# First attention of a four-block kernel: head outputs sent through DRAM to the output projection, full-array products moved to steps 5, 13, 21 and 29

## The reference

```python
x = x + attn(layernorm(x), qkv_w, qkv_b, proj_w, proj_b)   # 16 batches of 512 tokens, C = 128

H, D = 16, 8
qkv = (x @ qkv_w + qkv_b).reshape(b, n, 3, H, D)
attn = softmax(einsum('bnhd,bmhd->bhnm', q, k) * D ** -0.5, axis=-1)
out = einsum('bhnm,bmhd->bnhd', attn, v).reshape(b, n, 128)
out = out @ proj_w + proj_b
```

## Time and profile before

| | us |
|---|---|
| median of 3 runs | 3264.02 (3258.78 to 3268.07) |
| the profiled execution's own time | 3287.01 |
| its span, first to last instruction | 3285.2 |
| mean granted clock of PE | 0.905 of 2.4 GHz |
| PE busy in the span | 2902.0 |
| DVE busy in the span | 2549.6 |
| ACT busy in the span | 1791.8 |
| POOL busy in the span | 919.2 |

### The profile page before, as it was taken

One profiled execution on the slowest core, in us unless ns is written; L12 is line 12 of the kernel. 1 busy time (PEld: TensorE's weight loads), 2 busy tenths in 40 slices (PEclk: granted clock), 3 DMA queues, 4 the chain that ended last, 5 costly groups with the idle time before them and its releaser, 6 DMA issues. The chain is left out here.

```text
span 3285.2 us, 47363 instructions
## 1 busy us (share of the span) xinstructions
PE 2902.0 (88%) x15778; PEld 1773.0 (54%) x15778; DVE 2549.6 (78%) x6662; ACT 1791.8 (55%) x3223; POOL 919.2 (28%) x885
## 2 busy tenths in 40 slices
PE   6999879999999998999976698899899999989753
PEld 4666534444444443666644565566566656556432
DVE  7998768989989871899967898776476687697765
ACT  3544307778877774445445455464345555655444
POOL 2212121211211101122101555565233323434233
PEclk9999958999999996999985789899899999999965
DMA  4434322222212201344420000000000000000000
GB/s 130 101 83 104 81 98 95 76 77 95 86 67 95 83 25 52 79 104 94 89 52 1 1 14 20 13 26 20 33 10 11 14 14 7 14 7 26 7 7 26
DMA packets 71611, 167.26 MB, mean 51 GB/s; under 512 B 8792, under 2 KB 9416, under 8 KB 67144
## 3 DMA queue, kind: packets, MB, share of 16 engines
q1 hardware_dynamic: 69192, 160.04, 17.0%
q10 hardware_dynamic: 2176, 4.19, 0.3%
HBM read 120.68 MB, written 43.52 MB: 50 GB/s over the span
## 5 line engine op out<-in xcount | busy, mean ns | idle before, releaser
L697 DVE TENSOR_REDUCE att_mx<-att_s 128x1 f32<-128x512 f32 x1024 | 636.9, 683 | 92.6 <-PE att_s L949 91.7
L874 ACT ACTIVATE att_pt<-att_t 128x512 f32<-128x512 f32 x1024 | 548.5, 603 | 183.7 <-PE att_t L959 181.4
L949 PE MATMUL att_s<-att_k,att_q 32*128 32x512 f32 x1024 | 333.1, 532 | 31.2 <-DVE att_mx L697 16.0
L970 PE MATMUL att_o<-att_pt,att_vx 128*32 128x256 f32 x4096 | 335.8, 414 | 10.5 <-ACT att_oT L880 9.6
L959 PE MATMUL att_t<-att_q,att_k 32*128 32x512 f32 x1024 | 321.1, 521 | 2.9 <-ACT att_pt L874 2.6
L959 PEld LDWEIGHTS att_t<-att_q,att_k 32*128 32x128 f32 x1024 | 135.2, 190 | 217.5 <-ACT att_pt L874 106.5
L949 PEld LDWEIGHTS att_s<-att_k,att_q 32*128 32x128 f32 x1024 | 143.6, 194 | 69.8 <-DVE att_mx L697 51.3
L460 ACT ACTIVATE ffnA_h<-ffnA_up,b 128x512 f32<-128x512 f32 x144 | 98.6, 686 | 131.5 <-PE ffnA_up L105 131.0
L460 ACT ACTIVATE ffnB_h<-ffnB_up,b 128x512 f32<-128x512 f32 x144 | 98.6, 686 | 130.5 <-PE ffnB_up L105 130.0
L970 PEld LDWEIGHTS att_o<-att_pt,att_vx 128*32 128x32 f32 x4096 | 92.1, 112 | 143.4 <-ACT att_pt L874 70.3
L1896 ACT ACTIVATE att1k_sq<-att1k_k 128x512 f32<-128x512 f32 x128 | 76.1, 595 | 167.1 <-PE att1k_k L105 167.0
(11 more groups left out here) (535 smaller groups left out, 7710.7 us busy)
## 6 DMA issues: line engine op xcount, KB each, us to landing
ffnA_weights<-ffnA_weights SPq DMA_DIRECT2D x128, 256.0 KB, 5.3
att_q<-att_spread_q SPq DMA_DIRECT2D x16, 1024.0 KB, 5.0
att_k<-att_spread_k SPq DMA_DIRECT2D x16, 1024.0 KB, 4.8
att_spread_q<-att_qhi SPq DMA_DIRECT2D x32, 256.0 KB, 2.5
att_spread_k<-att_khi SPq DMA_DIRECT2D x32, 256.0 KB, 4.0
twk_hi<-ffnB_weights SPq DMA_DIRECT2D x32, 256.0 KB, 4.0
twk_lo<-ffnB_weights SPq DMA_DIRECT2D x32, 256.0 KB, 5.2
tgk_hi<-ffnB_weights SPq DMA_DIRECT2D x32, 256.0 KB, 6.1
```

Source lines behind the costliest of these rows:

```text
L697: v.tensor_reduce(top[b % 2][:, t, h + n % 2:h + n % 2 + 1], sbanks[n % 3][:, :], AX, ALU.max, negate=True).then_inc(mx, 1)
L874: a.activation(pt[k % 8][:, n % 2, :], tbanks[n % 3][:, :], ACT.Exp, scale=scale).then_inc(p_, 1)
L949: pe.matmul(sbanks[n % 3][:, :], qb[b % 3][r, u, t * P:(t + 1) * P], kb[b % 3][r, u, :], start=True, stop=True).then_inc(s_, 1)
L970: last = pe.matmul(obank[j * BLOCK:(j + 1) * BLOCK, cols], vxb[b % 3][:, t, 4 * u + j, :], pt[(2 * g + j // 2) % 8][:, j % 2, cols], start ...
```

## The change

The outputs of a unit no longer go back to tokens through PE. SP writes ACT's copy (values and sums of four heads, 256 KB) to a DRAM tensor `kept_o`, four times for a batch. When all four are there, SP loads the sums of the 16 heads as 128x64 (`rec`) and the values as channels by tokens (`ocol`). DVE inverts the sums in step 23. SP writes the inverses to DRAM and loads them again, each row repeated for the 8 channels of its head (`spread_rec`). POOL multiplies `ocol` by it, and PE projects at step 29, `ended` following at step 30. Values are computed at step 21 in place of 17, ACT's copy of them at 22 in place of 18. In stretches that have no next batch, PE gets two 128x512 products of constants into `misc` at steps 5, 13 and 21, which nothing reads.

```diff
+INVERTED = 23
-        def divided(w):
-            ...
-            m = st.at(v.reciprocal(rc[:, :, :], ov[:, :, :, HDIM]))
-            v.tensor_tensor(o[:, :, 4 * u:4 * u + 4, :], ov[:, :, :, 0:HDIM], ..., ALU.mult).then_inc(on, 1)
+        def inverted_sums(b):
+            v.wait_ge(sums, 16 * (b + 1))
+            if b:
+                v.wait_ge(inverted, 16 * b)
+            v.reciprocal(rec[:, :], rec[:, :]).then_inc(inverse, 1)
 # vector: loop over n
-                if n == 8 and old: divided(UNITS * (m - 2) + 2)
-                if n == 16 and old: divided(UNITS * (m - 2) + 3)
+                if n == INVERTED and old: inverted_sums(m - 2)
-                if n == 24 and old: ended(m - 2)
-                if n == 26 and now: divided(UNITS * (m - 1))
-                if n == 31 and now: divided(UNITS * (m - 1) + 1)
+                if n == 30 and old: ended(m - 2)
 # pool
-        for b in range(groups):
-            normal(b)
-            spread(b)
+        def divided(b):
+            p.wait_ge(came, 16 * (b + 1))
+            p.wait_ge(divisor, 16 * (b + 1))
+            p.tensor_tensor(ocol[:, :], ocol[:, :], spread_rec[:, :], ALU.mult).then_inc(on, 1)
+        for m in range(-1, groups + 2):
+            if m + 1 < groups:
+                normal(m + 1)
+                spread(m + 1)
+            if m >= 2:
+                divided(m - 2)
 # sync
+        def outputs(w):
+            b, u = divmod(w, UNITS)
+            sp.wait_ge(oT, w + 1)
+            if u == 0 and b:
+                sp.wait_ge(came, 16 * b)
+                sp.wait_ge(sums, 16 * b)
+            sp.dma_start(kept_o[4 * u:4 * u + 4, :, :]..., oTb[w % 2][:, :]).then_inc(kept[w % 2], 16)
+        def gather(b):
+            for written in kept:
+                sp.wait_ge(written, 16 * UNITS // 2 * (b + 1))
+            sp.dma_start(rec[:, :], kept_o[:, HDIM, :]...).then_inc(sums, 16)
+            if b:
+                sp.wait_ge(fp, b)
+            sp.dma_start(ocol[:, :], kept_o[:, 0:HDIM, :]).then_inc(came, 16)
+        def invert(b):
+            sp.wait_ge(inverse, b + 1)
+            if b:
+                sp.wait_ge(divisor, 16 * b)
+            sp.dma_start(kept_rec..., rec[:, :]).then_inc(inverted, 16)
+            sp.wait_ge(inverted, 16 * (b + 1))
+            sp.dma_start(spread_rec[:, :], kept_rec.unsqueeze(1).to_broadcast([HEADS, HDIM, GROUP])).then_inc(divisor, 16)
+        for m in range(groups + 2):
+            new, old, now = m + 1 < groups, m >= 2, 1 <= m <= groups
+            if now: maxima(m - 1)
+            if old: outputs(UNITS * (m - 2) + 2)
+            if new: operand_q(m + 1)
+            if old: outputs(UNITS * (m - 2) + 3)
+            if new: operand_k(m + 1)
+            if old:
+                gather(m - 2)
+                invert(m - 2)
+            if now:
+                outputs(UNITS * (m - 1))
+                outputs(UNITS * (m - 1) + 1)
 # scalar
-                a.wait_ge(oTT, w - 1)
+                a.wait_ge(kept[w % 2], 16 * (w // 2))
-                if n == 18 and new: values(m + 1)
+                if n == 22 and new: values(m + 1)
-                if n == 22 and old: final(m - 2)
 # tensor
+    def kept_busy(m, n):
+        return m + 1 >= groups and n in (5, 13, 21) and STEPS * m + n - LAG < total
+        def constant(k):
+            misc_free(pe, "constant", k)
+            for _ in range(2):
+                pe.matmul(misc[:, :], K["spread"][:, 0, :], K["spread"][:, 0:4, :]..., start=True, stop=True)
-                if n == 7 and old: out(UNITS * (m - 2) + 2)
-                if n == 15 and old: out(UNITS * (m - 2) + 3)
-                if n == 17 and new: project_v(m + 1)
-                if n == 21 and old: final(m - 2)
-                if n == 23 and old: projected(m - 2)
-                if n == 25 and now: out(UNITS * (m - 1))
-                if n == 30 and now: out(UNITS * (m - 1) + 1)
+                if n == 21 and new: project_v(m + 1)
+                if kept_busy(m, n): constant(STEPS * m + n)
+                if n == 29 and old: projected(m - 2)
```

More of the change, by code:

```diff
@@ L599, in attn0 @@
     total = STEPS * groups
-    (var, root, normed, biased, xT, xc, qp, kp, qr, kr, ql, kl, vp, vx, s_, mx, mt, mT, mr, t_, p_, w_, oT, oTT, on,
-     fT, fc, fp, done) = signals(nc, ctx, name, "var root normed biased xT xc qp kp qr kr ql kl vp vx s mx mt mT mr t p w oT oTT"
-                                 " on fT fc fp done")
+    (var, root, normed, biased, xT, xc, qp, kp, qr, kr, ql, kl, vp, vx, s_, mx, mt, mT, mr, t_, p_, w_, oT, on,
+     fp, done) = signals(nc, ctx, name, "var root normed biased xT xc qp kp qr kr ql kl vp vx s mx mt mT mr t p w oT on fp done")
+    kept = signals(nc, ctx, name, "kept0 kept1")
+    came, sums, inverse, inverted, divisor = signals(nc, ctx, name, "came sums inverse inverted divisor")
     dq, dk, dm = [signals(nc, ctx, name, f"{n}0 {n}1 {n}2") for n in ("dq", "dk", "dm")]
@@ L624, in attn0 @@
     spread_m = nc.dram_tensor(name + "_spread_m", [4, BLOCK, GROUP], F32, kind="Internal").ap()
+    kept_o = nc.dram_tensor(name + "_kept_o", [HEADS, BLOCK, GROUP], F32, kind="Internal").ap()
+    kept_rec = nc.dram_tensor(name + "_kept_rec", [HEADS, GROUP], F32, kind="Internal").ap()
     xg = lambda b: X[:, b, :, :]
@@ L639, in uses_of_misc @@
                 yield "x", m + 1
-            if old:
-                yield "out", UNITS * (m - 2) + 2
-            if new:
                 yield "q", m + 1
                 yield "k", m + 1
+                yield "v", m + 1
+            for n in (5, 13, 21):
+                if kept_busy(m, n):
+                    yield "constant", STEPS * m + n
             if old:
[L646 to L650, removed]
                 yield "proj", m - 2
-            if now:
-                yield "out", UNITS * (m - 1)
-                yield "out", UNITS * (m - 1) + 1
     misc_uses = list(uses_of_misc())
@@ L672, in misc_free @@
                 pe.wait_ge(mr, k + 1)
[L673 to L676, removed]
             if kind == "proj":
@@ L747, in vector @@
                     maxima(m - 1)
[L748 to L751, removed]
+                if n == INVERTED and old:
+                    inverted_sums(m - 2)
                 if n == 20 and m + 2 < groups:
@@ L755, in vector @@
                     stats(m + 2, 2, TILES)
[L756 to L759, removed]
                 if n == 29 and m + 2 < groups:
                     moments(m + 2)
-                if n == 31 and now:
-                    divided(UNITS * (m - 1) + 1)
+                if n == 30 and old:
+                    ended(m - 2)
     def pool(p):
@@ L909, in scalar @@
                     raw_k(m + 1)
-                if n == 18 and new:
+                if n == 22 and new:
                     values(m + 1)
@@ L913, in scalar @@
                     out(UNITS * (m - 1))
-                if n == 22 and old:
-                    final(m - 2)
                 if n == 29 and now:
@@ L978, in maxima @@
             last.then_inc(mT, 1)
[L980 to L988, removed]
+        def constant(k):
+            misc_free(pe, "constant", k)
+            for _ in range(2):
+                pe.matmul(misc[:, :], K["spread"][:, 0, :], K["spread"][:, 0:4, :].rearrange("p c n -> p (c n)"), start=True, stop=True)
         def projected(b):
-            pe.wait_ge(fc, b + 1)
+            pe.wait_ge(on, b + 1)
             misc_free(pe, "proj", b)
@@ L1017, in tensor @@
                     turned(m + 1)
-                if n == 7 and old:
-                    out(UNITS * (m - 2) + 2)
                 if n == 9 and new:
@@ L1023, in tensor @@
                     project_k(m + 1)
-                if n == 15 and old:
-                    out(UNITS * (m - 2) + 3)
-                if n == 17 and new:
+                if n == 21 and new:
                     project_v(m + 1)
-                if n == 21 and old:
-                    final(m - 2)
-                if n == 23 and old:
+                if kept_busy(m, n):
+                    constant(STEPS * m + n)
+                if n == 29 and old:
                     projected(m - 2)
[L1032 to L1035, removed]
     with nc.Block() as block:
```

45 lines of the change are left out of this document (20 added, 25 removed).

## The result

| | before | after |
|---|---|---|
| median of the runs, us | 3262.47 (3258.78 to 3268.07, 4 runs) | 3314.99 (3314.22 to 3318.98, 4 runs) |
| profiled execution, us | 3287.01 | 3315.72 |
| span, us | 3285.2 | 3313.8 |

The ratio of the runs is 1.0162, 95% interval 1.0144 to 1.018: +52.5 us, where I forecast +22 and a range up to 3314. The two profiles alone, 3315.7 and 3287.0, differ by only 28.7 us. That is the first thing to explain, and the second profile of before (experiment 1) does it.

What follows compares the result with a forecast made beforehand. DVE, and full-array work PE puts between scores, were taken to bound a stretch. Stretches +26, m = 15 -2, part without scores -11, tail +8, first stretches +1 gave +22 on 3264.0: 3286 us, range 3218 to 3314.

Steps and rivals of the forecast that it cites:

- (e): SP's DMAs: the sums land behind the k load, so DVE waits 2.9 us at step 23 (bounds 0.1 and 3.5).
- (g): Collisions in before's mean stretch of 48.71, 1.0 us; half kept, so 50.7 us a stretch, +26 us over thirteen.
- (a): DVE in m = 2 to 14: four pairs of L719 and L721 go, -2.0 us; the new reciprocal adds 0.3.
- (b): PE in m = 2 to 14: transposes leave, two full products move to steps 21 and 29: -1.4 us a stretch.
- (c): ACT loses `final` (0.6 us) but is not the bound: 0.
- (f): PE's clock falls with each wait at step 23: 2.7 us more a stretch, 50.2 us.
- (d): POOL's added 128x512 multiply, nearest row 1.28 us, stays hidden if it ends before PE's step 29.
- (h): Spread of the inverses to step 29: 7.1 us behind step 23, covered by six steps, 7.4 us: 0.
- End of the stage: After the thirteen stretches: m = 15 -2 us, the part without scores -11, the tail +8.
- R1: Rival, faster: the sums come in time and no stretch waits, 3213 us; chance 0.22.
- R2: Rival, about the same: DVE waits but the clock holds, 3251 us, up to 3260; chance 0.15.
- R3: Rival, clearly slower: a late multiply slides POOL's norm and L786 against L709, 3321 us; chance 0.08.

Runs made afterwards that it cites:

- experiment 1: The kernel before, unchanged, profiled a second time: 3265.91 us, span 3264.1, 47.76 us a stretch.
- experiment 8: Experiment 7's kernel with DVE's moments of the next batch at step 24 in place of 29: 3212.9 us, 0.9847 of before.
- experiment 7: Experiment 3's kernel with the q load also moved, behind the loads of sums and outputs and ahead of the inverses' write: 3224.56 us.
- experiment 6: The changed kernel with the load of the sums issued on ACT's queue at step 22 instead of SP's: 3289.84 us.
- experiment 5: The changed kernel with twenty 128x512 products of constants on PE at the end of step 23, in stretches with a next batch: 3285.06 us.
- experiment 2: The changed kernel with the loads of sums and outputs ahead of the k load, the inverses' write still behind it: 3269.96 us, 1.0012 of before.
- 9: The changed kernel with DVE's inversion at step 26 in place of 23: 3288.3 us.
- experiment 4: The changed kernel without the products of constants at steps 5, 13 and 21: 3326.3 us.
- experiment 3: The changed kernel with the k load behind all four transfers of the sums, outputs and inverses: 3221.7 us, 0.9876 of before.

## Why the prediction was wrong, point by point

The direction and the mechanism were right: DVE waits for the sums behind the k load in thirteen stretches and the clock falls with each wait. The size was wrong, +22 where the medians give +52.5. The step that failed is the size of the wait in (e), 2.9 us a stretch where 4.86 were measured, 25.5 us over the thirteen; next to it stands the base from which the stretches were counted, 12 us. The start and the end of the stage took 9.5 us more off than I had. By the windows of the changed kernel and of experiment 1, the spans differ by 49.7 us: start 2.4, thirteen stretches 63.2, m = 15 -3.6, without scores -21.6, tail 9.1, rest 0.2.

The first in order is the base, under "Sum" and in (g). I took the thirteen stretches as 13 x (50.7 - 48.71) = +26 and then added the same +22 to the median of the runs, "it lies 23 us over the median". More than half of the 23 us, 12.4 by the two profiles, were the 1.0 us a stretch that I subtracted. Against the ordinary stretch of 47.76 the same 50.7 give 13 x 2.94 = +38: 12 us of the miss. What (g) kept of the collisions, 0.5 us, did not come either: L705 took at most 367 ns in the changed kernel.

- **(a), (b): right.** 44.6 us if nothing waits; the kernel of experiment 8 has 44.85. The inversion, for which I took 0.3 us between two rows, took 0.55.
- **(c): right** as far as seen: ACT ends no wait in the rows above.
- **(e): right in kind, and the size is the step that failed.** 4.86 us of wait against 2.9, 13 x 2.0 = 25 us. DVE came 32.5 us after the start of the stretch (I had 32.0), so the difference is the landing: 37.3 us after it, against 34.9. I left the issue of the k load where it was, 29.7 us into the stretch. It moved to 31.7 on average, since the write of unit 3 and the k writes stand behind the 1 MB q load. The former took 6.3 us and more, the k writes 5.0 to 7.3 us and not 4.2 (2.4 to 3.8 in experiment 7, with no q load ahead), and "that eats the 0.5 us" was too little. And the k load itself took 5.4 us, with 256 KB of outputs issued behind it, not 4.8. My upper bound for the wait, 3.5 us, had no row for either. And SP's one queue, through which (e) has everything go in order, is not needed for it: the large load issued ahead is enough (experiment 6).
- **(f): right in size.** 2.7 us taken, 2.3 by experiment 5, 2.9 by what is left of 52.62 - 44.85 - 4.86.
- **(d), (h): right**, with its condition. The projection of step 29 waits for nothing in the changed kernel, since the wait at step 23 delays PE by as much. With the sums in time and the inverses' write behind the k load (experiment 2), or the inversion later (9), the cover is gone and DVE waits behind PE's step 29, up to 4.0 us in the one and 3.2 in the other, as (h) says that it would.
- **End of the stage: wrong in size.** m = 15 fell by 3.6 us, not 2, and the part without scores by 21.6 (75.00 to 53.39), not 11: the clock stays at 1.00 throughout. By the windows of experiment 4 (70.30), 16.9 of the 21.6 are the constants and 4.7 the rest of the change. Half of "at most 22" was a choice without a row. The tail was right: +9.1, from +8.

So the errors are +12.4 (base), +25 (stretches: 25.5 wait, 3.4 the 0.26 us between 44.59 and 44.85, 2.7 clock, -6.5 collisions) and -9.5 (end and start), together about +28 on +22, which is the 49.7 of the spans; the 3 us from there to the +52.5 of the medians lie inside their interval.

**The rivals.** R1's premise, a small load that passes a large one, fell: 4.9 us at the median. With the loads in another order no stretch waits, and the kernel of experiment 8 takes 3212.9 us where R1 had 3213, but that the two meet is luck. R1 had -47 for the stretches and -4 for the rest; against experiment 1 the profile of experiment 8 has -38 (13 x -2.91), +2 ahead of them and -16 behind. The Trainium skill's fixed cost of about 2.0 us ("DMA: Bandwidth & Descriptors", anatomy of one DMA), which the page gives for DMAs that GpSimd issues and not SP, agrees where nothing large is ahead, 2.2 us at the median in experiment 3, and there alone. R2 (the clock holds) happened only with PE filled (experiment 5). R3 did not happen in the changed kernel. In the profiles of experiments 2, 3, 6 and 9 L705 met POOL's addition in four, three, three and two stretches; as the kernel before had three, none and four, nothing shows that the multiply ahead of the norm is the reason.

**What stays open.** Why experiment 4's medians give half of what its windows do, and what makes runs of experiments 3 and 7 differ by 16 to 30 us: the one trace of experiment 3, of its slowest run, has collisions and late sums; that of experiment 7 is of its fastest, and the slow ones were not traced.

## What to carry to other kernels

A small load on which an engine waits in order should be issued ahead of every large one, in time and not only in its queue: 32 KB took 2.2 us with nothing large ahead and 4.8 to 6.7 behind 1 MB. Here one load, k's, moved behind the four transfers of sums, outputs and inverses in SP's queue, turned a kernel 1.6% slower than before into one 1.2% faster, and with the q load and the moments moved 1.5%. When a sum is made from one profile and laid on the median of runs, first see whether the profile's own excess lies in the very stretches that are being subtracted; the undisturbed stretch of the trace was the better base. A wait that leaves PE idle can cost more than its length: 4.9 us here brought 2.3 us more of a slower clock, which twenty products that nothing reads gave back.

## What the runs showed that I had not expected

A 32 KB load waits for a 1 MB load issued 0.15 to 0.30 us earlier in another engine's queue, and its first piece of data starts when 93% or more of the large load's have (experiment 6). The inversion of 128x64 took 0.55 us, 0.26 for 128x16, and the load of 128x512 with each row repeated for eight partitions took 3.1 to 3.4 us in the changed kernel. Two waits of DVE of 0.97 us in experiment 3 were followed by a fall of the clock, both in stretches that had been disturbed before, while one of 1.62 in experiment 2 left it at 1.00 in the stretch shown. And the changed kernel, which waits in every stretch, is the steadiest of all: its four runs lie within 5 us, the four of each of the fast kernels of experiments 3 and 7 within 30 and 16.
